# Making the whole first-layer weights of the last turn from their two parts, in place of a second load

## The reference, cut to what matters

```python
e = jnp.stack([tbl_0[ids[:, 0]], ..., tbl_25[ids[:, 25]]], axis=1)
combined = jnp.concatenate([dense_features[:, None, :], sparse_features], axis=1)
interactions = jnp.einsum('bfd,bgd->bfg', combined, combined)
iu, ju = jnp.triu_indices(FEATURE_NUM, k=1)
z = interactions[:, iu, ju]
h = jnp.concatenate([z, r_dense_features], axis=1)
h = jnp.maximum(h @ W_top1 + b_top1, 0.0)
h = jnp.maximum(h @ W_top2 + b_top2, 0.0)
y = h @ W_top3
```

## Time and profile before

| | |
|---|---|
| runs | 403.59, 403.60, 402.62 us; median 403.59 |
| profiled execution | 403.27 us, of which the span from first to last instruction is 401.5 us |
| mean granted TensorE clock | 0.970 of full speed |
| PE (TensorE matmul) | busy 360.9 us, 90% of the span |
| PEld (TensorE weight load) | 340.3 us, 85% |
| DVE (VectorE) | 280.9 us, 70% |
| POOL (GpSimd) | 219.3 us, 55%, all but 0.2 us of it issuing gathers |
| ACT (ScalarE) | 159.7 us, 40% |
| DMA engines | 34.35 MB, 86 GB/s as a mean |

### The profile page before, as it was taken

How to read it: one execution, slowest core, us unless ns; L and a number is a source line. 1 busy time by engine, 2 the same in 40 slices (tenths; PEclk the granted TensorE clock), 3 DMA queues, 4 the chain that set the end, 5 groups by cost and what they waited for, 6 DMA issues and landing times. The chain is left out here.

```text
span 401.5 us, 14641 instructions
## 1 busy us (share of the span) xinstructions
PE 360.9 (90%) x6468; PEld 340.3 (85%) x6468; DVE 280.9 (70%) x196; ACT 159.7 (40%) x270; POOL 219.3 (55%) x228
## 2 busy tenths in 40 slices
PE   0999687998879999999999989988998989996995
PEld 0889677997679988999898988988898988995794
DVE  3999899964569656993799395974599295972040
ACT  2365632344502454334433443344423443434222
POOL 5756543766247663676546665466466655564200
PEclk9999968999969999999999999999999999999699
DMA  6999113311313113311323123311312123233100
GB/s 187 282 270 293 60 40 97 89 49 47 105 39 88 46 47 97 88 55 52 93 69 79 46 63 103 82 47 50 113 54 77 46 58 107 56 82 118 29 18 4
DMA packets 23135, 34.35 MB, mean 86 GB/s; under 512 B 6127, under 2 KB 14959, under 8 KB 23115
## 3 DMA queue, kind: packets, MB, share of 16 engines
q1 hardware_dynamic: 15762, 19.30, 16.9%
q0 software_dynamic: 7168, 14.69, 13.3%
q10 hardware_dynamic: 186, 0.09, 0.1%
HBM read 30.97 MB, written 0.01 MB: 77 GB/s over the span
## 5 line engine op out<-in xcount | busy, mean ns | idle before, releaser
L295 POOL DMA_INDIRECT rows<-table,idx x224 | 219.1, 978 | 154.7 <-issue 60.7
L323 DVE TENSOR_TENSOR onehot<-ids_b,psum 125x2048 fp32r<-125x2048 int16 x97 | 216.2, 2280 | 6.1 <-DMA ids_b<-hot_ids 5.7
L407 ACT ACTIVATE feats<-psum 128x512 f32<-128x512 f32 (+2 forms) x120 | 80.5, 709 | 144.1 <-PE psum L548 115.8
L548 PE MATMUL psum<-onehot,hot_hi 125*128 125x256 f32 x736 | 110.9, 295 | 1.3 <-issue 1.2
L548 PE MATMUL psum<-onehot,hot_lo 125*128 125x256 f32 x736 | 104.0, 285 | 0.0
L303 DVE COPY gram<-psum 26x416 f32<-26x416 f32 x64 | 37.4, 584 | 90.7 <-PE psum L574 89.2
L548 PEld LDWEIGHTS psum<-onehot,hot_hi 125*128 125x128 f32 x736 | 97.5, 195 | 2.9 <-issue 1.9
L548 PEld LDWEIGHTS psum<-onehot,hot_lo 125*128 125x128 f32 x736 | 96.0, 193 | 0.0
L574 PEld LDWEIGHTS psum<-feats 128*26 128x26 f32 x4096 | 40.3, 103 | 18.5 <-issue 14.7
L574 PE MATMUL psum<-feats 128*26 128x26 f32 x4096 | 44.8, 193 | 12.4 <-issue 9.6
L563 PE MATMUL psum<-ident_sb,rows 128*128 128x128 f32 x240 | 38.8, 286 | 12.2 <-issue 9.0
(11 more groups left out here) (36 smaller groups left out, 169.9 us busy)
## 6 DMA issues: line engine op xcount, KB each, us to landing
lows<-table SPq DMA_DIRECT2D x12, 448.0 KB
ids_b<-hot_ids SPq DMA_DIRECT2D x8, 512.0 KB, 3.8
rows<-table,idx POOLq DMA_INDIRECT x224, 2.5
ids_b<-hot_ids SPq DMA_DIRECT2D x8, 256.0 KB, 3.7
lows<-w SPq DMA_DIRECT2D x2, 1024.0 KB, 15.0
rows<-dense SPq DMA_DIRECT2D x16, 64.0 KB, 3.3
lows<-table SPq DMA_DIRECT2D x12, 52.0 KB
pairs<-gram SPq DMA_DIRECT2D x16, 39.0 KB
```

The lines of the kernel that those rows point to most:

```text
L295: pool.indirect_dma_start(out=rows[:, f, :], out_offset=None, in_=tables[f - 1], in_offset=bass.IndirectOffsetOnAxis(ap=idx[:, 2 * s + t, ...
L323: nc.vector.tensor_tensor(onehot[f % SLOTS][0:HP_ROWS, :, :], ids_b[0:HP_ROWS, f:f + 1, :].to_broadcast([HP_ROWS, HC, SB]), psum[0:HP_ROWS ...
L407: return nc.scalar.activation(o, x, ACT.Copy)
L548: mm = nc.tensor.matmul(psum[:, bank, m * SB:(m + 1) * SB], part[0:HP_ROWS, f, c, :], onehot[f % SLOTS][0:HP_ROWS, c, :], start=(part is h ...
```

## The change

Turn 7's load of `w1_whole` from HBM (1 MB) goes. VectorE makes it instead, as `w1_hi` + `w1_lo`, between the gram copies of half 0 and `copy_dense`. TensorE's wait at the head of `last_layers` is for that sum instead of for the load.

```diff
@@ SyncE, in the turn loop
                 if s + 1 < TURNS:
                     load_ids(s + 1, 0)
-                else:
-                    sp.wait_ge(hot_done, NH * TURNS)
-                    sp.dma_start(w1_whole, w1.rearrange("(c p) n -> p c n", p=P)).then_inc(whole_w1_in, 16)
                 wait_gram(s, 0)
@@ VectorE, in turn()
                 if last:
+
+                    dve.wait_ge(hot_done, NH * TURNS)
+                    nc.vector.tensor_tensor(w1_whole.rearrange("p c n -> p (c n)"),
+                                            w1_hi[:, :, :].rearrange("p c n -> p (c n)").bitcast(fp32),
+                                            w1_lo[:, :, :].rearrange("p c n -> p (c n)").bitcast(fp32),
+                                            ALU.add).then_inc(w1_whole_made, 1)
                     copy_dense(s)
@@ TensorE, last_layers()
-                pe.wait_ge(whole_w1_in, 16)
+                pe.wait_ge(w1_whole_made, 1)
```

More of the change, by code:

```diff
@@ L152, in dlrm_tower @@
         stored = sem("stored")
-        whole_w1_in = sem("whole_w1_in")
+        w1_whole_made = sem("w1_whole_made")
         last_layer1_done = [sem(f"last_layer1_done{t}") for t in range(2)]
```

## The result

| | before | changed |
|---|---|---|
| median of 16 runs | 403.08 us (399.86 to 405.39) | 399.51 us (395.38 to 406.66) |
| profiled execution | 403.27 us, span 401.5 | 395.38 us, span 393.6 |
| ratio | | 0.987, interval 0.9835 to 0.9905 |

The changed kernel is faster, by 5.2 us going by the ratio. The ratio leaves out runs over 1.5% above the kernel's fastest; since the changed kernel scatters more widely, the medians of all runs differ by only 3.6 us. The forecast was 402.8 us, in a range of 400.0 to 404.0. The 16 times of before spread over 5.5 us; the three that I knew when I predicted spread over 1.0 us, so I took the noise for smaller than it is.

The account below looks back on a forecast made before the run. The prediction took TensorE's 4.82 us stall in turn 7, behind gathers the load delays, as the place to gain: 2.10 us saved, 1.57 lost to the held gather, TensorE 1.0 earlier, worth 0.5 at half speed; 403.27 - 0.5 = 402.8 us, range 400.0 to 404.0.

Parts of the forecast that it names:

- What bounds the kernel now: Turn 7: TensorE idles 4.82 us before the transposes of (1, 2), behind gathers that the 1 MB weights' load disturbs.
- The clock's share: Turn 7, 372.27 to 377.98: TensorE's work ran at half speed, which cost 2.85 us.
- What is removed: Turn 7: without the load the gather of 359.68 lands after 2.5 us, and bunch (1, 2) starts 2.10 us earlier.
- What is added: VectorE's sum, 366.08 to 368.37, lies in idle time but holds D: price 1.57 us of the 2.10.
- D: Fourth gather of bunch (1, 2) in turn 7; forecast to start at 366.67 and end at 369.18, not 367.61.
- The hold itself: A gather that starts while VectorE's two-input instruction runs is held until that instruction's end plus 0.81 us.
- One already under way is not: A gather begun before VectorE's instruction is not held; in turn 5 one 0.37 us old kept its 0.94 us.
- The clock: TensorE resumes 1.0 us earlier, but at half speed that is worth 0.5 us (0.25 to 0.7).
- cases 1 and 2: D held: clock falls before TensorE resumes, gain 0.25 to 0.7, chance 0.47; or falls after, gain 2.3, chance 0.20.
- rival 4: D not held, ends at 367.61; TensorE gains 2.1 to 3.0 us; 397.4 to 398.3 without slow stretch; chance 0.13.
- The forecast case: D held, clock falls before TensorE resumes, long slow stretch: 402.0 to 403.6 us, centred on 402.8; chance 0.47.

Follow-up runs that it names:

- sum_pieces_b: Changed kernel with its sum in four instructions of 128 x 512, rerun on a chip of usual speed: 399.76 us, ratio 0.987 to before.
- late1_sum_early: Changed kernel with turn 7's bunch (1, 1) forced to start after the last but one hot matmul: 403.56 us, ratio 1.0051 to before.

## Why the prediction was wrong

- **What bounds the kernel now**: right. The stall before (1, 2) was the load's, through the gathers of (1, 1), and removing or moving the load removes it. The clock's share, reckoned as 2.85 us, measured 2.68.
- **What is removed**: right in size. The gather issued third in bunch (1, 1) landed after 2.4 us, and the idle time before (1, 2) fell to 1.01 us; 2.1 us saved.
- **What is added, the step that failed**: "D would start at 366.67, 0.59 us into the add." In the changed kernel it started 1.88 us ahead of the sum. Counted from turn 7's first hot matmul, D started at 30.20 us and not at 31.35, and the sum at 32.08 and not at 30.76. Two terms were off. First, I took the place of bunch (1, 1) from one trace, in which it came at 21.87 us. In the traces on chips of usual speed where nothing forced that bunch, it came at 20.3 to 20.8 in seven, and late, at 21.6 to 21.9, in three; what makes it early or late is open. Second, I took the end of the gram copies over from a trace in which no gather started inside that gram. With the gathers running beside it the gram takes 3.45 us and not 2.38, and the copies began 0.75 us behind its end and not 0.12, which no run explains. So the sum came 6.57 us behind the gram's start and not 4.93. The trace of before could have warned me: in its turns 2 to 6, where gathers did start inside the gram of half 0, that gram took 2.92 to 3.79 us. With D clear of the sum and the gram longer, D landed before TensorE wanted it: no stall was left, the clock did not fall, and the trace gained 5.47 us in place of 0.5.
- **The hold itself**: its end, 0.81 us behind VectorE's instruction, was right within 0.02 us in seven traces. "One already under way is not" was wrong near the edge: gathers 0.16, 0.18 and 0.42 us old were held in full, the last on the chip of 468 us, while the one of 0.37 us in the earlier trace rows was not. Where the edge lies is open. The Trainium skill (SBUF — State Buffer, section Who interferes with whom) infers that such an instruction doesn't stall descriptor generation; 2.5 to 3.5 us gathers beside the sum contradict that for these gathers.
- **The clock**: cases 1 and 2 needed a stall. Where one was left, the second layer took 4.97 to 6.08 us, so both lengths of the slow stretch do occur, but in the usual place there was no stall. Where D was held (sum_pieces_b and late1_sum_early), the stall was 4.75 and 4.93 us and not 3.9: counted from the first hot matmul, D's hold ended 0.80 and 0.58 us later than reckoned, and TensorE went on 2.58 and 2.96 us behind its end, where I had taken about 2.1.
- **The chances**: rival 4, D not held, had 0.13, and its end without a fall of the clock, 397.4 to 398.3 us, was left out of the range. It is nearest to what the traces of the changed kernel show, and its gain of 5.0 to 5.9 us fits the measured 5.47 in part by luck: it kept 1.8 to 2.7 us of the stall, where nothing was left, and had neither the longer gram nor the wait of 1.15 us. The forecast case is real but, by the places seen, the rarer one. That it makes the changed kernel's long executions, up to 406.66 us, is likely and not shown, since none of them was traced.

## What to carry to other kernels

A transfer that nobody waits for can still be the stall, when it runs beside small transfers that an engine does wait for; look for landings that stretch while it is in flight, and try it at another place before you replace it. When an edit puts two engines' instructions near each other, read the distance from several executions and recompute it with every term that the edit itself changes; one trace gives a place, not its spread. A VectorE instruction with two SBUF inputs belongs where no gather on the path is being issued, as behind `copy_dense` here.

## What the runs showed of the hardware

- The 256 short matmuls of turn 7's gram of half 0 took 2.36 to 2.38 us in the four traces of the table in which no gather started inside it, 2.92 to 3.07 in the three with one, and 3.45 to 3.51 in the seven with two. With the bunch made to wait for the gram, it was 2.36. In the trace of before the 1 MB load was in flight over the whole gram of 2.38 us, so a transfer alone did not slow it. In the changed kernel some 85 of the gram's matmuls ran in the 0.35 us up to 359.35, with the DMA engines 49 to 88% busy, and some 31 in the 0.40 us from 359.60, while a gather was being issued and no DMA moved. That points at the issue of gathers; by what way it slows TensorE is open.
- Two gathers issued while the 1 MB load was in flight landed after 5.1 and 4.6 us, against a median of 2.5.
- A hold goes on over back-to-back VectorE instructions of 0.6 us each: 3.48 us for one gather.
- One chip took 468.36 us for the kernel that takes 402 to 404 on the others, by medians.
